# Four-layer graph and transformer kernel: weight loads moved behind row transfers, other PSUM banks for the first keys, and half of a norm moved to ScalarE

## The reference

```python
hg = jnp.einsum('bnf,gf->bng', h3, Wg[:, :F])
qg = jnp.einsum('blf,gf->blg', q, Wg[:, F:]) + bg
attn = jax.nn.sigmoid(hg[:, :, None, :] + qg[:, None, :, :])
qi = jnp.einsum('bnlf,blf->bnf', attn, q)
```

```python
merged = jnp.where(attn_mask[..., None], attn_out, mix_out)
h = hidden_states + merged
n2 = _ln(h, g2, b2)
ffn = jax.nn.gelu(n2 @ W1 + bf1, approximate=False) @ W2 + bf2
return h + ffn
```

## Time and profile before

| What | Value |
|---|---|
| median of 3 runs | 1323.51 us (1323.05 to 1326.19) |
| the profiled execution | 1323.78 us |
| its span | 1322.0 us |
| TensorE / weight load busy | 97% / 85% |
| VectorE / ScalarE / GpSimd busy | 74% / 59% / 16% |
| mean granted TensorE clock | 0.994 |
| HBM over the span | 142 GB/s |

### The profile page before, as it was taken

One profiled execution on the slowest core, in us unless ns is written; L12 is line 12 of the kernel. 1 busy time (PEld: TensorE's weight loads), 2 busy tenths in 40 slices (PEclk: granted clock), 3 DMA queues, 4 the chain that ended last, 5 costly groups with the idle time before them and its releaser, 6 DMA issues.

```text
span 1322.0 us, 24350 instructions
## 1 busy us (share of the span) xinstructions
PE 1282.2 (97%) x10110; PEld 1119.5 (85%) x10110; DVE 978.1 (74%) x1772; ACT 784.2 (59%) x1301; POOL 216.5 (16%) x108
## 2 busy tenths in 40 slices
PE   9999999999999989999999999999999999999998
PEld 8999644699844589889988999889999999998986
DVE  8775777865777788788788668867676777789555
ACT  3455898645698756566656565645455554547344
POOL 0210587300297500002121001010000000000100
PEclk9999999999999999999999999999999999998999
DMA  9276159136157334053365461534455555233200
GB/s 365 73 252 198 54 130 289 43 138 199 42 143 237 100 132 156 33 203 106 139 239 176 152 212 60 195 130 154 169 179 182 186 188 195 78 126 149 84 1 25
DMA packets 31121, 195.35 MB, mean 148 GB/s; under 512 B 4241, under 2 KB 4370, under 8 KB 15011
## 3 DMA queue, kind: packets, MB, share of 16 engines
q1 hardware_dynamic: 31010, 193.79, 43.6%
HBM read 183.55 MB, written 3.93 MB: 142 GB/s over the span
## 4 chain that ended last, share of the span: by engine, by line
PE 79%; DVE 9%; ACT 6%; DMA 4%; issue 1%; POOL 1%; SPq 0%; POOLq 0%; DVEq 0%; ACTq 0%
PE PS L370 65%; PE PS L1182 4%; DMA RT<-AS 3%; PE PS L1191 3%; PE PS L375 3%; ACT PS L1291 2%; PE PS L777 2%; DVE WK L1351 1%; DVE WL L313 1%; ACT WH L306 1%; PE PS L1604 1%; PE PS L552 1%; DVE SM L634 1%; ACT WK L1288 1%; ACT WK L2182 1%
## 5 line engine op out<-in xcount | busy, mean ns | idle before, releaser
L313 DVE TENSOR_TENSOR WL<-w,WH 128x768 fp32r<-128x768 f32 x366 | 351.9, 972 | 152.1 <-ACT WH L306 150.5
L306 ACT ACTIVATE WH<-w 128x768 fp32r<-128x768 f32 x381 | 315.6, 840 | 238.8 <-PE PS L370 232.2
L370 PE MATMUL PS<-XS,WH 128*128 128x256 f32 x2256 | 408.4, 284 | 2.4 <-DVE XS L584 1.4
L370 PEld LDWEIGHTS PS<-XS,WH 128*128 128x128 f32 x2256 | 347.8, 189 | 7.2 <-issue 2.8
L370 PE MATMUL PS<-XS,WL 128*128 128x256 f32 x1128 | 317.9, 282 | 0.0
L370 PEld LDWEIGHTS PS<-XS,WL 128*128 128x128 f32 x1128 | 213.1, 189 | 0.0
L1351 DVE TENSOR_TENSOR WK<-PS,WK 128x1024 f32<-128x1024 f32 x128 | 151.4, 1220 | 47.2 <-ACT PS L1291 43.2
L1433 POOL TENSOR_TENSOR WK<-WK 128x1024 f32<-128x1024 f32 x62 | 148.2, 2395 | 183.7 <-ACT WK L1288 183.6
L370 PE MATMUL PS<-WH,GS 128*128 128x256 f32 x864 | 159.9, 284 | 0.9 <-DVE GS L584 0.9
L1291 ACT ACTIVATE PS<-PS 128x1024 f32<-128x1024 f32 x130 | 125.6, 1008 | 26.8 <-PE PS L1182 26.8
L370 PEld LDWEIGHTS PS<-WH,GS 128*128 128x128 f32 x864 | 135.5, 190 | 2.7 <-DVE GS L584 1.4
(11 more groups left out here) (303 smaller groups left out, 2075.8 us busy)
## 6 DMA issues: line engine op xcount, KB each, us to landing
w<-f2W_in SPq DMA_DIRECT2D x40, 1152.0 KB, 5.4
w<-Wrel_in SPq DMA_DIRECT2D x12, 1152.0 KB, 7.1
WK<-qrep_in SPq DMA_DIRECT2D x16, 768.0 KB, 6.4
w<-f1Wi_in SPq DMA_DIRECT2D x8, 1152.0 KB, 6.1
w<-f1Wo_in SPq DMA_DIRECT2D x8, 1152.0 KB, 5.2
w<-f3Wqkv_in SPq DMA_DIRECT2D x6, 1152.0 KB, 15.3
RT<-qg_rows SPq DMA_DIRECT2D x16, 384.0 KB, 6.8
RT<-AS SPq DMA_DIRECT2D x32, 192.0 KB, 6.6
```

The source lines that it names most:

```text
L306: A.e.activation(w_hi(i), w_raw(i), ACT.Copy).then_inc(*hi("w", i))
L313: V.e.tensor_tensor(w_lo(i), w_raw(i), w_hi(i), ALU.subtract).then_inc(*lo("w", i))
L370: ins = T.e.matmul(o, l, r, start=i == 0 and first, stop=i == n - 1 and last, skip_group_check=lint)
```

## The change

1. In both gates SyncE first waits until the queries and rows of block 5 have landed, and then issues the two weight units that stood right behind their issue; likewise for block 6.
2. In the last layer the key tiles 0 to 5 go to banks 7, 0, 4, 5, 4, 5 and no longer to 4, 5, 6, 7, 4, 5.
3. In the pooling layer the first half of the second norm is done on ScalarE by `half_move`, with VectorE's `half_scale` in the last `om_out`. The bridges have 6, 2 and 5 matmuls for 4, 5 and 5. The two additions of `hx` to x move behind all three lower halves of the GELU's result; they were behind the first and the third.

```diff
-BRIDGE = {"gate": (2, 3), "f0c": (4, 5, 5), ...}
+BRIDGE = {"gate": (2, 3), "f0c": (6, 2, 5), ...}
...
                 rows_h(b)
-                if b == 5:
-                    load_units(nxt + 6)
-                if b == 6:
-                    load_units(nxt + 12)
+                if b in (5, 6):
+                    L.wait_ge(qin[b % 2], n, b)
+                    L.wait_ge(gin[b % 2], n, b)
+                    load_units(nxt + 6 if b == 5 else nxt + 12)
...
             bridge("f0c", 0, 0)
-            half_turn("f0c", 0, (0, 1, 2))
+            half_turn("f0c", 0, (0, 1, 2), True)
...
             half_sqrt("f0c", 0)
+            half_move("f0c", xn3, hx)
             half_sqrt("f0c", 1)
...
-            def om_out(m, c0, c1):
+            def om_out(m, c0, c1, scale=False):
...
                                   ALU.add).then_inc(*vec("hx", c0, m))
+                if scale:
+                    half_scale("f0c")
                 V.wait_ge(vec, "hx", c0, m)
...
             for m in range(2):
-                om_out(m, 512, 768)
+                om_out(m, 512, 768, m == 1)
                 half_ln("f0c", m)
-                half_norm("f0c", m, hx)
+            half_norm("f0c", 1, hx)
...
                 vec_lower(GH[0][:, 1, k, :], gtmp[:, k, :], GH[0][:, 0, k, :], "gelu", "f0", k)
-                if k != 1:
-                    m = k // 2
-                    V.e.tensor_tensor(x3[:, m, :], x3[:, m, :], hx[:, m, :], ALU.add).then_inc(*vec("f0x", m))
+            for m in range(2):
+                V.e.tensor_tensor(x3[:, m, :], x3[:, m, :], hx[:, m, :], ALU.add).then_inc(*vec("f0x", m))
...
             pe_gemm_T("f3k", zk, 0, 6, xs_at, lambda f: (act, "f3k", f), None,
-                      lambda f: [(LB[:, 768 + f * P:768 + (f + 1) * P], adT)], (4, 5, 6, 7))
+                      lambda f: [(LB[:, 768 + f * P:768 + (f + 1) * P], adT)], (7, 0, 4, 5, 4, 5))
```

More of the change, by code:

```diff
@@ L26 @@
 WARM = (4, 8, 8, 8, 8, 6, 5)
-BRIDGE = {"gate": (2, 3), "f0c": (4, 5, 5), "g3": (4,), "f3": (2, 5), "one": (9, 14)}
+BRIDGE = {"gate": (2, 3), "f0c": (6, 2, 5), "g3": (4,), "f3": (2, 5), "one": (9, 14)}
 GADD = 6
```

## The result

The changed kernel took 1333.88 us (median of 6 runs, 1331.09 to 1336.91) against 1324.62 us before (6 runs), a ratio of 1.0076 with a 95% interval of [1.006, 1.0092]: slower by about 9.3 us. The forecast of 1325.4 us and its range up to 1329.5 missed it. Of all executions in this document one, of `late_all`, ran at a mean granted clock of 0.85 (1393.98 us); its trace is not read and its ratio is formed without it.

The account below looks back on a forecast made before the run. TensorE, busy for 97% of the span, was taken as the bound, so only its idle stretches could give. Gates +2.3, keys -0.9 and pooling layer +0.2 made +1.6 on 1323.78: 1325.4 us, 8-in-10 range 1320.2 to 1329.5.

Parts of the forecast that it names:

- part 1: Both gates, weight units held until the landing: 2.70 us of stalls go, 5.0 come; +2.3 us, bounds -2.5 and +5.9.
- The landing: Gates, blocks 5 to 7: rows land 8.3 us after a block's first DMA undisturbed, against block 5's 10.8 before.
- the free 9.87: Gates: time a block's rows have to land without a stall, 12.87 us block distance less 3.0 until issue.
- Block 7's stall: Each gate: landing after 8.3 + 2.4 + 1.7 = 12.4 us, a stall of 2.5 us, bounds 0.1 and 3.5.
- rival (b): Gates: block 7's longer stall halves the clock, 3.4 us lost per gate; 1328.8 us for one, 1332.2 for both; chance 0.14.
- Rival (a): Gates: rows pass the weights, blocks 5 to 7 lose all stalls; -3.2 us, 1320.5 us; chance 0.28.
- Rival (d): Whole kernel: stalls come out as large as before, pooling gives back the keys' gain; 1323.5 us, chance 0.12.
- Rival (c): Gates: strict order, block 5's 10.8 us its own; stalls 0.5, 2.0, 2.5 at blocks 5 to 7; 1330.4 us, chance 0.05.
- Part 2: Last layer's keys: TensorE's 0.93 us idle before the first key matmul goes; -0.9 us, bounds -0.95 and -0.5.
- Part 3: Pooling layer: norm half on ScalarE -0.35 us, moved additions +0.53; +0.2 us in all, bounds -0.6 and +1.0.
- The sum: Whole kernel: gates 2.3, keys -0.9, pooling layer 0.2, together +1.6 us on 1323.78, giving 1325.4 us.

Follow-up runs that it names:

- late_all: Changed kernel, but all four weight units of a gate issued only after block 7's queries and rows have landed: 1321.64 us, ratio 0.9969.
- late_keys: Kernel before with all four weight units issued after block 7's landing and the key tiles' new banks, without the norm: 1319.80 us, ratio 0.9965.
- late_only: Kernel before with one edit, all four weight units issued only after block 7's queries and rows have landed: 1320.31 us, ratio 0.9975.
- gate_only: Kernel before with only the gates' waits for blocks 5 and 6 ahead of their weight units: 1332.37 us, ratio 1.0053.
- no_gate: Changed kernel with the gates' old issue order, so only key banks and norm with its additions are changed: 1324.47 us, ratio 0.9995.
- wait6: Changed kernel with the wait for block 6 alone; block 5's units go out right behind its rows: 1325.88 us, ratio 1.0013.
- after_again: The changed kernel measured a second time, nothing altered: 1331.68 us, ratio 1.0057 to the kernel before.
- cover2: Changed kernel with empty matmuls before blocks 6 and 7, in the bank the `select` writes next: 1327.93 us, ratio 1.0038.
- wait5: Changed kernel with the wait for block 5 alone; block 6's units go out right behind its rows: 1326.48 us, ratio 1.0008.
- cover: Changed kernel with empty matmuls before blocks 6 and 7, in bank b % 2, which brought a wait of its own: 1332.31 us, ratio 1.0068.

## Why the prediction was wrong

Two terms of part 1 failed: a landing time, and the clock, which the sum put at nothing.

*The landing.* "From the first DMA of a block (1.56 us before the last) this is 8.1 to 8.3 us undisturbed, for which I take 8.3", used for blocks 5 to 7 alike. It was read from block 4, and low even there: its last DMA went out 1.97 us behind its first, and it landed after 8.6 and 8.2 us. Block 7 does land in 8.3 to 8.5 us with nothing near (late_keys, late_only). But block 5, with no unit near it, took 9.6 and 9.9 us in the changed kernel, 9.4 and 9.8 in gate_only, and 8.1 to 10.5 (median 9.4) over 18 instances in nine traces. With two units behind it, it took 9.6 to 11.1 (median 10.6) in the six instances of before, no_gate and wait6. So the units behind cost it some 1.2 us on average, not the 2.5 of the sum, and the held-back units go out 1.2 to 1.5 us later than the sum had it. In its own arithmetic that puts 5.7 - 3.3 = 2.4 us of weights ahead of block 6 for 1.2, and 8.3 + 2.4 = 10.7 us is beyond the free 9.87. Measured were 11.4 and 10.9, stalls of 1.5 and 1.0 us where the forecast had 0 with a bound of 0.8. Why block 5 takes a microsecond more than the others with nothing beside it was not settled.

*Block 7's stall* came out near the forecast, 2.3 and 2.0 us for 2.5, but by luck. Its landing took 13.7 and 12.9 us where the forecast had 12.4, since block 6's late landing put the next units only 1.5 and 2.0 us ahead of it and not 3.3. Block 6's stall had given it 1.5 and 1.0 us more time than the 9.87 of the sum, and the two errors nearly cancel. Blocks 6 and 7 together lost 3.8 and 3.0 us a gate where 2.5 stood.

*The clock* was rival (b), which was given 0.14. It is real but not a threshold in length alone: a stall of 2.6 us in gate_only left the clock up, and stalls of 1.75 (no_gate) and 1.9 us (after_again) were followed by a fall. The price was 1.5, 1.5 and 2.4 us in the traces of the changed kernel and not 3.4, and it falls due in some executions only; the old order pays it at times too. The Trainium skill ("TensorE: Matmul & The Clock Gate", "HAM oscillation — how this bites in real kernels") describes waits on DMA that put the array back to half rate. The traces agree, but the waits of its example are 3 to 5 us long, and here waits of about 2 us were enough. cover2 shows the way out, work that computes nothing in the wait.

*Rival (a)* fell: with the units issued 3.3 us or less in front, no block of the changed kernel landed unharmed. *Rival (d)*, no change, is outside the interval. *Rival (c)* was nearer than its 0.05. Its premise, that block 5's landing is mostly its own, held for some 9.4 of 10.6 us, and its shape of stalls at 6 and 7 is what came; its 2.0 and 2.5 us were 1.5 and 1.0 and 2.3 and 2.0, and the 0.5 that it left at block 5 was 0 in the first trace, 0.2 in after_again and 0.6 and 0.4 in wait5. The rule of the Trainium skill's page "DMA: Bandwidth & Descriptors" ("Queues, rings and completion order"), that each engine starts a ring's descriptors in order, is borne out for work ahead. That work behind should then cost nothing is not: block 5 landed some 1.2 us later with two units behind it than with none, though the two ranges overlap. (wait5's block 6, with units behind as well, landed later too, after 14.7 and 11.5 us for 11.4 and 10.9, but there the units ahead were also 0.5 to 0.9 us closer.)

*Part 2* went the forecast way: the idle stretch went and came back nowhere. But -1.2 us is beyond its bound of -0.95, as the idle time was read from the modelled end of the matmuls before. *Part 3* was right step by step: -0.3 for -0.35 at the `f0u` matmuls, then +0.45 for +0.53 behind the additions, +0.1 for +0.2 in all.

*The sum.* The first profiled execution has stalls of 1.5 + 1.0 + 2.3 + 2.0 = 6.8, less 2.7, plus 1.5 for the clock, or +5.6 for part 1 where +2.3 stood. That is still under the upper bound of 5.9, but the medians of gate_only say +8.0, beyond it. In after_again's trace the stalls are 9.1 us and two clock falls 3.9. So stalls and falls vary from one execution to the next. An estimate that takes the stalls of each trace less 2.7, less 1.1 for parts 2 and 3 where they are in, plus what the mean clock of its executions lacks beyond the 8.1 us of before, gives +8.4 for the changed kernel, +8.0 for gate_only, +9.2 for after_again, +8.4 for cover and +3.3 for cover2. Measured were +9.3, +8.0, +8.1, +6.9 and +4.4. Stalls and clock are thus about as large as the loss. The executions' mean clocks do not tell where in them the clock fell; only the traces do, and of the changed gates there are three.

## What to carry over

A transfer that nobody needs soon does harm both ahead of an urgent one and behind it. When it is held back, ask where it lands in the sequence of urgent ones that follow: here the wait took 0.5 us a gate off block 5 and raised what blocks 6 and 7 lost from 0.8 to 3.4 us, while one block further on, behind the last urgent transfer, the same bytes cost nothing and the kernel gained 3 to 6 us.

A landing time read from one transfer is not that of its neighbours: take the free time as a margin only if several instances show it. And a TensorE stall of some 2 us in dense work is priced with the clock behind it, on average over executions, not only with its own length. Where each block has its own time of issue, price the landing of the last one, not each stall by itself: an early stall is time that a later one need not pay.

## What the hardware showed

The same 1.57 MB of a block (queries 768 KB, rows 384 and two of 192) landed, with no weight unit in flight, in 8.3 to 8.5 us for block 7 and in 8.1 to 10.5 for block 5; blocks 2 to 4 took 8.0 to 9.1 in the twelve traces that are read. The same stalled `select` was put down to VectorE in one trace and to the DMA in another; the queue's next issue, at 219.36 for 219.35 and 217.63 for 217.62, settles it. And with empty matmuls of 1.4 and 2 us in the waits the granted clock stayed at 1.00 in each of the four gates that had them, and the mean clock was 0.9935 over 17 executions for 0.9908 over 21 without.
